# A decoder layer on one Trainium2 core: the query, key and value products as three passes of high and low parts

## The reference, cut to what matters

```python
xn = layernorm(x, g1)            # of an already normalised x; g1 scales the columns
q = xn @ Wq.T                    # 256 -> 1024
kv = xn @ Wkv.T                  # 256 -> 128: key and value
q, k = l2norm(q), l2norm(k)      # then scaled, softmax(q k^T), times v
```

## Time and profile before

| | |
|---|---|
| median of 3 runs | 998.96 us (996.46 to 1001.12) |
| profiled execution, own time | 1001.04 us |
| its span, first to last instruction | 999.3 us |
| PE busy | 882.3 us, 88% of the span |
| DVE busy | 612.9 us, 61% |
| ACT busy | 562.5 us, 56% |
| mean granted TensorE clock | 0.939 of full speed |

### The profile page before, as it was taken

The page is one execution under the profiler, slowest core; times in us unless marked ns, Lnnn a source line. Parts: engine busy times, 40 slices in busy tenths (PEclk is TensorE's granted clock), DMA queues, the critical chain, the costliest instruction groups (busy, mean ns, idle before and its releaser), DMA issues.

```text
span 999.3 us, 14240 instructions
## 1 busy us (share of the span) xinstructions
PE 882.3 (88%) x4366; PEld 669.0 (67%) x4366; DVE 612.9 (61%) x1417; ACT 562.5 (56%) x1112; POOL 203.9 (20%) x220
## 2 busy tenths in 40 slices
PE   4699898999999897999989999999760299999997
PEld 2467676777777675776776777777550178888885
DVE  4667758667858677668766778778766133323231
ACT  1478667677867577667758678768442022222221
POOL 3212321302112121212313020201103401111111
PEclk9699999999999999999989999999955599999999
DMA  8300000020000000000000003200232201010100
GB/s 283 71 1 1 1 1 1 1 85 1 1 2 0 1 2 0 2 1 0 2 1 1 1 1 107 63 1 1 85 127 72 81 1 32 20 32 21 32 17 9
DMA packets 19175, 29.01 MB, mean 29 GB/s; under 512 B 2079, under 2 KB 15648, under 8 KB 19104
## 3 DMA queue, kind: packets, MB, share of 16 engines
q1 hardware_dynamic: 17008, 22.73, 7.5%
q0 software_dynamic: 1680, 4.21, 1.2%
q10 hardware_dynamic: 416, 1.18, 0.3%
HBM read 21.41 MB, written 7.10 MB: 29 GB/s over the span
## 4 chain that ended last, share of the span: by engine, by line
PE 49%; DVE 6%; issue 5%; POOL 3%; ACT 2%; DMA 1%; DVEq 0%; ACTq 0%; POOLq 0%
PE W L1418 7%; PE S L1395 6%; PE O L1395 5%; PE O L1235 3%; PE O L1232 3%; PE S L1217 3%; PE S L1216 3%; PE O L1233 3%; PE W L1306 3%; PE W L1348 3%; PE W L1274 2%; PE W L1328 2%; POOL sorted_rows L700 2%; PE W L1336 1%; PE W L1361 1%
## 5 line engine op out<-in xcount | busy, mean ns | idle before, releaser
L944 DVE TENSOR_TENSOR pl<-pr,ph 128x512 fp32r<-128x512 f32 x288 | 200.2, 698 | 72.4 <-ACT pr L750 64.4
L749 ACT ACTIVATE ph<-S 128x512 fp32r<-128x512 f32 x288 | 173.7, 603 | 107.5 <-PE S L1217 105.2
L750 ACT ACTIVATE pr<-S 128x512 f32<-128x512 f32 x288 | 172.7, 600 | 0.0
L1232 PE MATMUL O<-ph,vhi 128*65 128x512 f32 x288 | 145.1, 504 | 0.0
L1235 PE MATMUL O<-pl,vhi 128*65 128x512 f32 x288 | 116.3, 404 | 8.2 <-DVE pl L944 7.8
L1217 PE MATMUL S<-qT,kT 128*128 128x512 f32 x288 | 115.3, 400 | 0.0
L1216 PE MATMUL S<-qT,kT 128*128 128x512 f32 x288 | 115.0, 399 | 0.0
L1233 PE MATMUL O<-ph,vlo 128*65 128x512 f32 x288 | 114.7, 398 | 0.0
L651 POOL TENSOR_TENSOR rs<-ri,half 128x1 f32<-128x1 f32 x48 | 34.9, 727 | 306.0 <-DVE ri L883 306.0
L1274 PE MATMUL W<-wqkv,zT 128*128 128x384 f32 x192 | 75.5, 527 | 3.8 <-DVE qT L996 1.6
L858 ACT ACTIVATE gate<-S 128x512 f32<-128x512 f32 x38 | 20.6, 596 | 102.8 <-PE S L1395 102.8
(11 more groups left out here) (174 smaller groups left out, 1637.8 us busy)
## 6 DMA issues: line engine op xcount, KB each, us to landing
raw<-in_w_v SPq DMA_DIRECT2D x16, 512.0 KB, 4.0
wps<-in_w_proj SPq DMA_DIRECT2D x4, 1024.0 KB, 10.1
sorted_rows<-pad_row SPq DMA_DIRECT2D x19, 128.5 KB, 4.3
xs<-sorted_rows SPq DMA_DIRECT2D x19, 128.5 KB, 2.0
wqkv<-in_wqkv_t ACTq DMA_DIRECT2D x1, 1152.0 KB, 6.3
wout<-in_wout_t SPq DMA_DIRECT2D x1, 1024.0 KB, 10.0
xall<-in_x SPq DMA_DIRECT2D x1, 1024.0 KB, 10.3
xall<-in_x SPq DMA_DIRECT2D x1, 768.0 KB, 7.8
```

The source lines that it names most:

```text
L749: nc.scalar.activation(ph[:, k % RING, :], S[k % AHEAD][:], ACT.Exp, scale=SIM_SCALE).then_inc(ph_ready, 1)
L750: nc.scalar.activation(pr[:, k % RING, :], S[k % AHEAD][:], ACT.Exp, scale=SIM_SCALE)\
L944: nc.vector.tensor_tensor(pl[:, k % RING, :], pr[:, k % RING, :], ph[:, k % RING, :].bitcast(F32), ALU.subtract).then_inc(pl_ready, 1)
L1232: nc.tensor.matmul(o, vhi[:, vs, 0:DH + 1], ph[:, k % RING, :], start=j == 0, stop=False)
```

## The change

The qkv product becomes three float32r passes for each half of the 256 rows: high rows by high weights, high rows by low weights, low rows by high weights, so six matmuls of 384 columns for each job in place of two in float32. For this:

- The weights come into a buffer `wstage` that lies in the memory of the ring `pr`, `ph`. ACT writes the scaled high part (two activations of 1152 columns, rounded to float32r), DVE the scaled low part (two operations that multiply and subtract); `wqkv` is twice as large.
- ACT copies the transposed rows to `zTh` in float32r, and a new stage `z_low` on DVE subtracts it from the bank into `zTl`. The bank is freed by `z_low`, not by ACT's copy, and PE's qkv job waits for that.
- `z_low` stands at 12/33 of the slot. `q_turn` and `q_low` of parts 1 and 2 move one thirty-third back. `COST` of `qkv` on PE goes from 1.3 to 1.1, and `z_low` has 0.42 on DVE. `lows_early` and the planner's `fill` treat `z_low` as they do `q_low`.

```diff
-    ("norm_x", 0, 2, 7), ("heads_out", 0, 0, 9), ("z_turn", 0, 2, 11), ("q_turn", 1, 1, 11), ("q_low", 1, 1, 12),
-    ("q_turn", 2, 1, 14), ("q_low", 2, 1, 15), ("heads_out", 1, 0, 17), ("qkv", 0, 2, 19), ("qkv", 1, 2, 21),
+    ("norm_x", 0, 2, 7), ("heads_out", 0, 0, 9), ("z_turn", 0, 2, 11), ("z_low", 0, 2, 12), ("q_turn", 1, 1, 12), ("q_low", 1, 1, 13),
+    ("q_turn", 2, 1, 15), ("q_low", 2, 1, 16), ("heads_out", 1, 0, 17), ("qkv", 0, 2, 19), ("qkv", 1, 2, 21),
...
-    "kv": (0.4, 0, 0.4), "q_turn": (0, 1.2, 0.4), "qkv": (0, 0.48, 1.3), "qkv_squares": (0, 0.65, 0), "out_turn": (0, 0.6, 0.4),
+    "kv": (0.4, 0, 0.4), "q_turn": (0, 1.2, 0.4), "z_low": (0.42, 0, 0), "qkv": (0, 0.48, 1.1), "qkv_squares": (0, 0.65, 0), "out_turn": (0, 0.6, 0.4),
...
+LOWS = {"q_turn": "q_low", "z_turn": "z_low"}
...
-        zT = sb(early, "zT", [P, CH, P])
+        zTh = sb(early, "zTh", [P, CH, P], F32R)
+        zTl = sb(early, "zTl", [P, CH, P], F32R)
...
-        wqkv = sb(early, "wqkv", [P, CH, QKV])
+        wqkv = sb(early, "wqkv", [P, CH, 2, QKV], F32R)
...
+        first = ExitStack()
+        wstage = sb(first, "wstage", [P, CH, QKV])
+        first.close()
...
-            act.dma_start(wqkv[:], wqkv_t.rearrange("(c p) n -> p c n", p=P)).then_inc(w_in, 16)
+            act.dma_start(wstage[:], wqkv_t.rearrange("(c p) n -> p c n", p=P)).then_inc(w_in, 16)
+            act.wait_ge(w_in, 32)
+            for c in range(CH):
+                nc.scalar.activation(wqkv[:, c, 0, :], wstage[:, c, :], ACT.Identity, scale=g1c[:, c:c + 1]).then_inc(wqh_ready, 1)
...
-                        nc.scalar.copy(zT[:].rearrange("p c n -> p (c n)"), W[job % WB][:, 0:DIM]).then_inc(act_freed, 1)
+                        nc.scalar.copy(zTh[:].rearrange("p c n -> p (c n)"), W[job % WB][:, 0:DIM]).then_inc(zth_ready, 1)
...
-                nc.vector.tensor_scalar(wqkv[:, c, :], wqkv[:, c, :], g1c[:, c:c + 1], None, ALU.mult).then_inc(wq_scaled, 1)
+                dve.wait_ge(wqh_ready, c + 1)
+                nc.vector.scalar_tensor_tensor(out=wqkv[:, c, 1, :], in0=wstage[:, c, :], scalar=g1c[:, c:c + 1],
+                                               in1=wqkv[:, c, 0, :].bitcast(F32), op0=ALU.mult, op1=ALU.subtract)\
+                    .then_inc(wq_scaled, 1)
...
+                    elif name == "z_low":
+                        dve.wait_ge(zth_ready, t + 1)
+                        nc.vector.tensor_tensor(zTl[:].rearrange("p c n -> p (c n)"),
+                                                W[job_of["z_turn", 0, t] % WB][:, 0:DIM],
+                                                zTh[:].rearrange("p c n -> p (c n)").bitcast(F32), ALU.subtract)\
+                            .then_inc(dve_freed, 1)
...
-                        pe.wait_ge(act_freed, freed_count("z_turn", 0, t))
+                        pe.wait_ge(dve_freed, freed_count("z_turn", 0, t))
                         freed_wait(pe, job)
-                        for c in range(CH):
-                            mm = nc.tensor.matmul(W[job % WB][:, 0:QB], zT[:, c, :], wqkv[:, c, part * QB:(part + 1) * QB],
-                                                  start=c == 0, stop=c == CH - 1)
+                        passes = [(rows, lo, c) for c in range(CH) for rows, lo in ((zTh, 0), (zTh, 1), (zTl, 0))]
+                        for m, (rows, lo, c) in enumerate(passes):
+                            mm = nc.tensor.matmul(W[job % WB][:, 0:QB], rows[:, c, :],
+                                                  wqkv[:, c, lo, part * QB:(part + 1) * QB],
+                                                  start=m == 0, stop=m == len(passes) - 1)
```

More of the change, by code:

```diff
@@ L174, in lows_early @@
                 owed = [entry for entry in owed if entry[1] < WB]
-                if name == "q_turn":
-                    owed.append([("q_low", part, t), 0])
-            elif name == "q_low":
+                if name in LOWS:
+                    owed.append([(LOWS[name], part, t), 0])
+            elif name in LOWS.values():
                 owed = [entry for entry in owed if entry[0] != (name, part, t)]
@@ L191, in fill @@
     def fill(name, part, t):
-        if name == "q_low":
+        if name in LOWS.values():
             counts["dve"] += 1
-            freed[turned[part, t]] = ("dve", counts["dve"])
+            freed[turned[name, part, t]] = ("dve", counts["dve"])
         if name not in READER:
             return None
-        if name == "q_turn":
-            turned[part, t] = len(freed)
+        if name in LOWS:
+            turned[LOWS[name], part, t] = len(freed)
             freed.append(None)
@@ L443, in build @@
         dconst = sem("dconst")
+        wqh_ready = sem("wqh_ready")
         wq_scaled = sem("wq_scaled")
+        zth_ready = sem("zth_ready")
         side_ready = sem("side_ready")
```

## The result

The changed kernel takes 1006.46 us (median of ten runs, 1004.73 to 1008.77), the kernel before 997.23 over ten runs. The ratio is 1.0089, 95% interval 1.0076 to 1.0102: slower by 9.2 us, where 5.0 us less were forecast, and outside the forecast range of 987 to 1004. The profiled span is 1007.0 us in place of 999.3.

The account below looks back on a forecast made before the run. PE was taken to bound the kernel: -9.8 us from its passes, +1.7 start, +2.8 short slots, +0.3 long slots, in sum -5.0, from a median of 998.96 to 994.0 us; range 987 to 1004.

Parts of the forecast that it names:

- the long slots: Slots outside tiles 0, 1, 8 and 9: `z_low` hidden in DVE's idle time, later `q_turn` and `q_low` nothing; +0.3 us.
- its reckoning of tile 1: Slot of tile 1 in the start: `q_low` and first qkv job 1.6 late, 1.4 given back, net 0.2 us.
- the short slots: Eight-position slots of tiles 0, 1, 8, 9: `z_low` delays `q_low` and the product; +2.8 us, ends 0 and 6.
- What bounds the kernel: PE is mostly what the rest waits for; a microsecond of its work saved is nearly one of time.
- B: Rival: PE's freed time turns into waiting for DVE and ACT, half of 9.8 us kept; 998.9 us, chance 0.21.
- Pass for pass: qkv jobs on PE: six passes take 1.06 us in place of 1.29, 0.23 saved a job at full clock.
- A: Rival: qkv passes cost columns alone, 0.161 us each, net -8.1 us; 990.9 us, chance 0.13.
- C: Rival: a pass has a fixed floor, 0.233 us at 384 columns, job 1.40; +7.2 us, 1006, chance 0.07.
- The share of 0.9: Part of PE's 10.9 us saving that is realised, as PE shows some 5% idle; -9.8 us.
- The start: Tiles 0 and 1: weight split and `z_low` delay the first products, partly given back by faster passes; +1.7 us.
- D: Rival: `z_low` blocks DVE's queue in long slots too, PE waits for `pl`; +4.9 us, 1003.9, chance 0.13.
- The planner's costs: Planner: the lower `COST` puts some chain work a position later, nothing by itself on a PE-bound stretch.

Follow-up runs that it names:

- experiment 9: Experiment 2 with its chain held and `q_low` of parts 1 and 2 alone one thirty-third later; 1021.91 us, ratio 1.0262.
- experiment 6: Changed kernel with old places of `q_turn` and `q_low`, `z_low` behind them, chain held as in the changed kernel; 989.33 us, ratio 0.9922.
- experiment 2: Changed kernel with the planner's old costs and old places, `z_low` behind `q_low` part 1; 990.40 us, ratio 0.9922.
- experiment 10: Experiment 2 with its chain held and `q_turn` of parts 1 and 2 alone one thirty-third later; 986.87 us, ratio 0.9891.
- Experiment 7: Experiment 2 without `z_low`: third pass takes the high rows again, bank freed by ACT's copy; 989.70 us, ratio 0.9915.
- experiment 8: Changed kernel with `z_low` alone moved behind `q_low` part 1, chain and all else held; 1000.96 us, ratio 1.0032.
- experiment 5: Changed kernel with its new places kept, the chain behind the attention held at the positions of experiment 2; 1014.15 us, ratio 1.0168.
- experiment 11: Kernel before, old product, its chain held, `q_turn` and `q_low` of parts 1 and 2 one thirty-third later; 1012.38 us, ratio 1.0139.
- experiment 1: Kernel before, old arithmetic, with the changed kernel's planned places and costs, no engine acting on `z_low`; 1002.11 us, ratio 1.0057.

## Why the prediction was wrong

**The step that failed** is a term put at nothing, in the paragraph on the long slots: "`q_turn` and `q_low` of parts 1 and 2 one thirty-third later: the scores that need them come half a slot after, nothing." It asked who reads `qT`, and not who waits for the bank that `q_low` frees. The reader has half a slot; the bank's next user is the third side job on, and PE stands in its queue there. Moving `q_low` alone cost 31 us, moving `q_turn` alone nothing (3.5 less), and moving both under the old product 14.

The prediction did see this bank in its reckoning of tile 1 ("The first qkv job needs that `q_low`'s bank"), and it reckoned with a late `q_low` in the short slots, 2.8 us in all. But it priced it as a delay of the product. In the slot of tile 0 that is what came (PE waits 2.8 us ahead of the product, 1.0 before). In those of tiles 1, 8 and 9 the wait was met a job earlier, at `q_turn` part 2. It occurs in long slots too (4.0 us once in the slot of tile 6 of experiment 9). Beside experiment 6, which has the same chain and the old places, the changed kernel's span is 19.7 us longer: 10.3 of it in the four short slots, 2.2 in the start, 5.8 in the long slots 2 to 7 and 10 to 13, and 1.3 in the rest. So the sentence was wrong for the slots under which it stands, and the term of the short slots was too small by more.

**What bounds the kernel.** Right that PE does; B, in which its freed time turns to waiting, had a half of the gain come back. What came was not freed time in waiting but a new wait.

**Pass for pass.** Right: 1.05 to 1.11 a job against 1.06. A, columns alone, would have been 0.97. C's floor of 1.40 is out. A pass of 0.175 to 0.18 is also above the 0.1625 that the Trainium skill gives (TensorE: Matmul & The Clock Gate, Back-to-back issue gap), so here the trace does not agree with it at 384 columns either. By that figure the prediction's sum would have been, as an estimate, 3.1 us better and not 3.5 (39 jobs of six passes, 0.0145 each, times 0.9).

**The share of 0.9 and the sum.** With the old plan the change gives 5.6 us (experiment 2), 7.8 (experiment 6) and, with `q_turn` alone later, 11 (experiment 10), against 5.0 forecast. The arithmetic was sized right or a little low; how much of the spread is the plan and how much the passes is not told apart. That the sum fits the old plan does not make the forecast right: it was for the change with its own plan.

**The start.** Forecast 1.7 late, measured 3.0 (the first value pass at 41.0 for 38.0; with the old plan of experiment 2 it is 1.5 late). The first product at 13.75 and tile 1's at 33.18 are right. What failed is the 1.4 us given back in tile 1: its eighteen passes ran at half clock almost to the end, and took 5.8 us where twelve records, at mixed clock, had 5.4.

**The long slots.** Each of 2 to 7 and 10 to 13 was to be 0.6 us or so shorter. One by one they are not (3 and 13 are 1.3 and 7.2 longer, 7 and 12 are 4.3 and 7.5 shorter), as the chain's stages moved between them; in sum they are 9.2 shorter.

**The short slots.** 1.2 each was forecast for tiles 0 and 8; the slot of tile 0 grew by 0.7, that of tile 1 by 3.0 where 0.2 was forecast, and those of 8 and 9 by 4.4 together. In all that is 8.1 us against 2.8, beyond the end of 6 that the prediction gave the term.

**`z_low`.** Experiment 7 bears out that it is hidden when `q_low` is ahead of it. D, `z_low` blocking DVE for `pl`, named the right queue and the wrong victim: PE's waits for `pl` are 8.6 us in 10 after, 7.8 in 9 before, while those for `q_low` went from 11.8 to 22.7. D's condition, DVE waiting for ACT's `zTh`, is there (6.4 us in 8), and experiment 8 gave 5.5 us for putting `z_low` behind. It acts through banks: it makes `q_low` late, and where it stands behind, PE waits for the bank that `z_low` itself frees.

**The planner's costs.** The chain was to move "a position later"; it moved by 3.65 on average. "Nothing by itself" holds with the old places (experiment 6). With the new places the new chain is even better than the old: experiment 5 to the changed kernel is 8 us, and experiment 11 to experiment 1 is 10. Why is open; of the waits in the table, 2.2 us fall away in the first pair and 3.9 in the second.

## What to carry to other kernels

When a stage moves in a list that engines run in order, ask two questions of it, not one: who reads what it writes, and who waits for the buffer that it frees. In a ring of three banks the second comes soon, and it stops the whole queue of the engine that stands there. A faster product came in with a retimed plan here. Timing the two apart showed that the product gives 6 to 8 us at the old places, and that the two effects do not simply add: the plan costs 6 us with the old product and 16 with the new one. Where the granted clock falls along with the waits, a wait costs more than its length; here 8 us of them in two slots came with 12 us of time.

## What the runs showed of the hardware

A single float32r pass of 384 columns takes 0.175 us at full clock and 0.32 at half clock, between 0.16 for the same columns in float32 (a record of 384 takes 0.32 and counts as two) and 0.23 for 512 columns in float32r. So the extra over the columns that the steps' passes have is there at 384 columns too, about 0.015 us, and the float32 records do not have it.

A `scalar_tensor_tensor` into float32r takes about 1.37 us for 1152 columns (two in 2.75); 1.35 had been reckoned from the subtraction of two tensors. The old scaling, in place and with one tensor read, had two in 1.55.
